# Feed-forward 0: small quantisation rows in PSUM, x first in VectorE's turn, statistics and factors in pairs, bank 0 shared

## What is computed

```
_GRID = [0.0, 0.5, 1.0, 1.5, 2.0, 3.0, 4.0, 6.0]; _MID = [0.25, 0.75, 1.25, 1.75, 2.5, 3.5, 5.0]
def fp4_quant_dequant(x):                 # blocks of 16 along the last dimension
    scale = max(max(|xb|) / 6, 1e-12)
    return _GRID[searchsorted(_MID, |xb / scale|)] * sign(xb) * scale
def fp4_linear(x, w): return quant(x) @ quant(w).T
gate, y = fp4_linear(x, w_gate), fp4_linear(x, w_up)      # 128 -> 352
out = fp4_linear(silu(gate) * y, w_down)                  # 352 -> 128
...
x = x + gelu(attention0(layernorm(x)));  x = x + ffn0(layernorm(x))
x = x + attention1(layernorm(x));        x = x + ffn1(layernorm(x))
```

## Time and profile before

| | us |
|---|---|
| median of 3 runs (1053.13 to 1054.89) | 1053.9 |
| the profiled execution | 1056.3 |
| its span | 1054.6 |
| PE busy in the span | 904.9 (86%) |
| DVE busy | 779.8 (74%) |
| ACT busy | 527.1 (50%) |
| POOL busy | 473.3 (45%) |

### The profile page before, as it was taken

How to read it: one execution, slowest core, us unless ns; L and a number is a source line. 1 busy time by engine, 2 the same in 40 slices (tenths; PEclk the granted TensorE clock), 3 DMA queues, 4 the chain that set the end, 5 groups by cost and what they waited for, 6 DMA issues and landing times. The chain is left out here.

```text
span 1054.6 us, 18304 instructions
## 1 busy us (share of the span) xinstructions
PE 904.9 (86%) x6457; PEld 588.5 (56%) x6457; DVE 779.8 (74%) x1505; ACT 527.1 (50%) x782; POOL 473.3 (45%) x643
## 2 busy tenths in 40 slices
PE   4799999995577667648999999988879999999997
PEld 3666777664455544524444444444356677667765
DVE  6788888875778888568878888888676666566742
ACT  3577777795234334444777767765732231323221
POOL 4122222225455556642655664545435433444344
PEclk9999999998688998776999999999999999999999
DMA  9100000000000000364444443410000000000000
GB/s 292 32 11 11 10 10 10 10 1 4 1 1 11 0 1 11 83 138 106 104 103 94 105 103 82 106 46 3 13 11 1 21 21 20 0 20 20 10 10 10
DMA packets 35639, 43.34 MB, mean 41 GB/s; under 512 B 4826, under 2 KB 27770, under 8 KB 35570
## 3 DMA queue, kind: packets, MB, share of 16 engines
q1 hardware_dynamic: 35569, 42.43, 16.5%
HBM read 21.21 MB, written 15.07 MB: 34 GB/s over the span
## 5 line engine op out<-in xcount | busy, mean ns | idle before, releaser
L1589 ACT ACTIVATE PT<-PS 128x1024 f32<-128x1024 f32 x160 | 162.8, 1022 | 68.3 <-PE PS L1373 68.1
L1643 POOL TENSOR_SCALAR_AFFINE_SELECT PT<-PT 128x256 f32<-128x256 f32 (+1 forms) x224 | 97.1, 449 | 133.1 <-ACT PT L1589 131.6
L2044 POOL TENSOR_TENSOR PRE_sb<-PRE_sb,VA 128x512 f32<-128x512 f32 x64 | 82.3, 1287 | 140.3 <-DVE PRE_sb L2110 140.2
L2007 ACT ACTIVATE sg_d<-PS 128x512 f32<-128x512 f32 x64 | 38.2, 597 | 176.7 <-PE PS L1111 176.7
L369 ACT ACTIVATE E<-PS,m 128x512 f32<-128x512 f32 x128 | 86.7, 684 | 40.9 <-PE PS L291 32.0
L2110 DVE TENSOR_TENSOR PRE_sb<-sg_d,PS 128x512 f32<-128x512 f32 x64 | 43.3, 686 | 79.1 <-ACT sg_d L2007 77.8
L1680 DVE TENSOR_REDUCE negm<-PS 128x2 f32<-128x1024 f32 x64 | 78.0, 1224 | 23.4 <-PE PS L1362 21.8
L496 DVE TENSOR_SCALAR E<-E 128x512 f32<-128x512 f32 x128 | 70.3, 549 | 33.6 <-ACT E L369 29.5
L1358 PE MATMUL PS<-kS,qS 48*128 48x384 bf16 (+3 forms) x512 | 75.0, 316 | 22.7 <-DVE negm L1680 8.5
L1388 PE MATMUL PS<-PT,VA 128*32 128x512 f32 (+3 forms) x1024 | 90.9, 452 | 1.4 <-POOL PT L1643 1.4
L406 POOL TENSOR_SCALAR Qs<-Qs 128x1024 f32<-128x1024 f32 x32 | 35.4, 1108 | 113.5 <-ACT Qs L357 113.5
(11 more groups left out here) (297 smaller groups left out, 2318.4 us busy)
## 6 DMA issues: line engine op xcount, KB each, us to landing
qk_rows<-parts SPq DMA_DIRECT2D x32, 192.0 KB, 2.8
qS<-qk_rows SPq DMA_DIRECT2D x32, 192.0 KB, 4.3
kS<-qk_rows SPq DMA_DIRECT2D x32, 192.0 KB, 4.6
xs_sb<-XN_sb SPq DMA_DIRECT2D x23, 256.0 KB, 2.3
qk_rows<-parts SPq DMA_DIRECT2D x32, 128.0 KB, 2.8
X_sb<-in_x_dram SPq DMA_DIRECT2D x8, 256.0 KB, 6.7
qk_rows<-parts SPq DMA_DIRECT2D x32, 64.0 KB, 2.4
out_dram<-X_sb SPq DMA_DIRECT2D x8, 256.0 KB, 2.3
```

The costliest lines, as they stand in the source:

```text
L1589: nc.scalar.activation(PT[:, quad % 2, u, :], PS[:, b:b + 2, :].rearrange("p b n -> p (b n)"), ACT.Exp).then_inc(exp_ready, 1)
L1643: nc.gpsimd.affine_select(out=v, in_=v, pattern=[[0, 4 if u == 4 else 2], [1, P]], compare_op=ALU.is_ge, fill=0.0, base=0, channel_multipl ...
L2044: nc.gpsimd.tensor_tensor(acts[:, s, f, :], acts[:, s, f, :], W[:, slot, s, :], ALU.mult).then_inc(weighted, 1)
```

## The change

- `am` and `inv` of each quantisation, for x and both hidden halves, lie in PSUM bank 1. The scale row `sc` stays in SBUF.
- The down products go to bank 0, half a bank each, and are kept by half (`keep_out(i, half)`). The bank is now used in turn by the attention sum, the transposed x, the two down halves and, in the last turns, the projections.
- VectorE's turn is `make_h(i, 0)`, `quantise_x(i + 1)`, `quantise_h(i, 0)`, `make_h(i, 1)`, `stats_x(i + 2)`, `stats_out(i - 1)`, `aggregate`, `quantise_h(i, 1)`. The eight `bn_aggr` of the two statistics stand together behind one wait.
- GpSimd rescales x in one piece ahead of `rescale_h(i, 0)`, and makes both factors with one chain of four instructions on 8 columns.
- TensorE's and ScalarE's orders are written anew, with `sum_att(i + 3)` a block earlier and functions of their own for the last two turns.

```diff
-    def __init__(self, sb, name, n):
+    def __init__(self, sb, name, n, small=None):
         self.y, self.pw, self.mg = (sb(name + m, [P, n]) for m in ("_y", "_pw", "_mg"))
-        self.am, self.sc, self.inv = (sb(name + m, [P, n // QB]) for m in ("_am", "_sc", "_inv"))
+        self.sc = sb(name + "_sc", [P, n // QB])
+        self.am, self.inv = small or (sb(name + m, [P, n // QB]) for m in ("_am", "_inv"))
...
+        nx, nh = NT * D // QB, 2 * I0 // QB
+
+        q_x = Scratch(sb, "qx", NT * D, [PS[:, 1, k * nx:(k + 1) * nx] for k in range(2)])
+        q_h = [Scratch(sb, "qh%d" % half, 2 * I0, [PS[:, 1, 2 * nx + (2 * half + k) * nh:2 * nx + (2 * half + k + 1) * nh] for k in range(2)])
+               for half in range(2)]
+        shift, vare = sb("shift", [P, 2, NT]), sb("vare_b", [P, 2, NT])
...
-                    pe.wait_ge(xqT_ready, i * 2 - 2)
+                    pe.wait_ge(xqT_ready, i - 1)
...
-            def turn_xq(i, part):
+            def turn_xq(i):
+                pe.wait_ge(xq_ready, i + 1)
+                if i < 2:
                     pe.wait_ge(att_kept, i + 2)
-                for t in (2 * part, 2 * part + 1):
+                else:
+                    pe.wait_ge(out_kept, i * 2 - 2)
+                for t in range(NT):
                     ins = nc.tensor.transpose(PS[:, 0, t * P:(t + 1) * P], xq[:, t, :], ident[:])
                 ins.then_inc(xq_turned, 1)
...
             def down(i, half):
-
-                pe.wait_ge(att_kept, i + 1)
-                if half == 0 and i > 0:
-                    pe.wait_ge(out_kept, i)
                 for t in (2 * half, 2 * half + 1):
-                    nc.tensor.matmul(PS[:, 1, t * P:(t + 1) * P], ident[:], X[:, i * NT + t, :], start=True, stop=False)
+                    nc.tensor.matmul(PS[:, 0, t * P:(t + 1) * P], ident[:], X[:, i * NT + t, :], start=True, stop=False)
                     if t % 2 == 0:
                         pe.wait_ge(hqT_ready, (i * 2 + half) * 2 + 2)
                     for r, (k0, kn) in enumerate(KT0):
-                        ins = nc.tensor.matmul(PS[:, 1, t * P:(t + 1) * P], hqT[0:kn, t % 2, r, :], g.wdT[0:kn, r, :], start=False, stop=(r == 2))
+                        ins = nc.tensor.matmul(PS[:, 0, t * P:(t + 1) * P], hqT[0:kn, t % 2, r, :], g.wdT[0:kn, r, :], start=False, stop=(r == 2))
                 ins.then_inc(down_ready, 1)
 
             def turn(i):
                 gate_up(i, 1)
...
                 if i > 0:
                     turn_h(i - 1, 1)
...
+                    pe.wait_ge(out_kept, i * 2 - 1)
                     down(i - 1, 1)
...
+                turn_xq(i + 1)
+                if i + 3 <= LAST:
+                    sum_att(i + 3)
+                gate_up(i + 1, 0)
                 turn_h(i, 0)
+                if i + 3 <= LAST:
+                    pe.wait_ge(att_kept, i + 4)
+                else:
+                    pe.wait_ge(xqT_ready, i + 2)
                 down(i, 0)
...
+            def turn_before_last(i):
+                gate_up(i, 1)
+                turn_h(i - 1, 1)
+                pe.wait_ge(out_kept, i * 2 - 1)
+                down(i - 1, 1)
+                turn_xq(i + 1)
+                pe.wait_ge(xqT_ready, NB)
+                pr.turn_x(pe, 0)
+                gate_up(i + 1, 0)
+                pr.project(pe, 0, 0, g.wq1, pr.q_ready)
+                turn_h(i, 0)
+                pe.wait_ge(pr.qf_ready, 1)
+                down(i, 0)
+
+            def last_turn(i):
+                gate_up(i, 1)
+                pe.wait_ge(out_kept, i * 2 - 1)
+                pr.project(pe, 0, 0, g.wk1, pr.k_ready)
+                turn_h(i - 1, 1)
+                pe.wait_ge(pr.kf_ready, 1)
+                down(i - 1, 1)
+                pe.wait_ge(out_kept, i * 2)
+                pr.turn_x(pe, 1)
+                turn_h(i, 0)
+                pr.project(pe, 1, 1, g.wq1, pr.q_ready)
+                pe.wait_ge(pr.qf_ready, 2)
+                down(i, 0)
+                pe.wait_ge(out_kept, i * 2 + 1)
+                pr.project(pe, 1, 1, g.wk1, pr.k_ready)
+                turn_h(i, 1)
+                pe.wait_ge(pr.kf_ready, 2)
+                down(i, 1)
...
             sum_att(0)
             sum_att(1)
             pe.wait_ge(w_kept, 4)
-            turn_xq(0, 0)
+            turn_xq(0)
             gate_up(0, 0)
-            turn_xq(0, 1)
-            for i in range(NB):
+            sum_att(2)
+            for i in range(LAST - 1):
                 turn(i)
+            turn_before_last(LAST - 1)
+            last_turn(LAST)
...
+            def keep_out(i, half):
+                own = X[:, i * NT + 2 * half:i * NT + 2 * half + 2, :].rearrange("p a d -> p (a d)")
+                act.wait_ge(down_ready, i * 2 + half + 1)
+                nc.scalar.activation(own, PS[:, 0, 2 * half * P:2 * (half + 1) * P], ACT.Copy).then_inc(out_kept, 1)
+
+            def keep_xq(i):
+                act.wait_ge(xq_turned, i + 1)
+
+                if i > 0:
+                    act.wait_ge(up_ready, i * 2)
+                nc.scalar.activation(xqT[:, :], PS[:, 0, :], ACT.Copy).then_inc(xqT_ready, 1)
...
             def turn(i):
                 silu(i, 1)
...
                 if i > 0:
                     keep_h(i - 1, 1)
+                    keep_out(i - 1, 1)
+                keep_xq(i + 1)
+                if i + 3 <= LAST:
+                    keep_att(i + 3)
+                silu(i + 1, 0)
+                keep_h(i, 0)
                 if i + 2 <= LAST:
...
+                    norm_x(i + 2)
+                keep_out(i, 0)
                 if i > 0:
                     norm_out(i - 1)
...
+            def factor(event, done, k0, k1):
+
+                ch = Steps(pool, g.pool_steps_b, event, 3)
+                both = [P, k1 - k0, NT]
+
+                wait_apart(pool, g.turns_g, g.factor_ready, NB + done - (k1 - k0))
+                wait_apart(pool, g.turns_g, g.stats_ready, NB + done)
+                ch.link(nc.gpsimd.tensor_scalar(vare[:, k0:k1, :], g.mv[:, k0:k1, :, 1], EPS_LN, 1.0, ALU.add, ALU.mult))
+                ch.link(nc.gpsimd.tensor_tensor(g.factor[:, k0:k1, :], vare[:, k0:k1, :], g.mhalf[:].unsqueeze(1).broadcast_to(both), ALU.pow))
+                ch.step(nc.gpsimd.tensor_tensor(shift[:, k0:k1, :], g.mv[:, k0:k1, :, 0], g.factor[:, k0:k1, :], ALU.mult))
...
             def rescale_x(i):
                 pool.wait_ge(x_rounded, i + 1)
...
+                ch = Steps(pool, tail_steps, i, 1)
+                rescale(nc.gpsimd, ch, xq[:, :, :].rearrange("p t (b k) -> p (t b) k", k=QB), q_x).then_inc(xq_ready, 1)
+                ch.end()
...
             for i in range(LAST):
+                rescale_x(i + 1)
                 rescale_h(i, 0)
-                rescale_x(i + 1)
-                if i > 0:
-                    factor(i * 2 + 1, 1)
-                if i + 2 <= LAST:
-                    factor(i * 2 + 2, 0)
+                if i == 0:
+                    factor(2, 3, 0, 1)
+                elif i + 2 <= LAST:
+                    factor(i + 2, i * 2 + 3, 0, 2)
+                else:
+                    factor(NB, 2 * NB - 2, 1, 2)
                 rescale_h(i, 1)
...
+            def aggregate(k0, k1):
+                norm.wait()
+                for k in range(k0, k1):
+                    for t in range(NT):
+                        norm.step(nc.vector.bn_aggr(g.mv[:, k, t, :], g.st[:, k, t, :]))
+                norm.wait()
+                dve.sem_inc(g.stats_ready, k1 - k0)
...
             for i in range(NB):
                 make_h(i, 0)
+                if i < LAST:
+                    quantise_x(i + 1)
                 quantise_h(i, 0)
                 make_h(i, 1)
+                if i + 2 <= LAST:
+                    stats_x(i + 2)
                 if i > 0:
                     stats_out(i - 1)
-                if i < LAST:
-                    quantise_x(i + 1)
-                if i + 2 <= LAST:
-                    stats_x(i + 2)
+                aggregate(0 if i + 2 <= LAST else 1, 2 if i > 0 else 1)
                 quantise_h(i, 1)
             stats_out(LAST)
+            aggregate(1, 2)
```

More of the change, by code:

```diff
@@ L172 @@
 QSTEPS = 6
-XQ_STEPS = 2 * NT + QSTEPS
 def attention0(nc, g, w):
@@ L721, in gate_up @@
             def gate_up(i, half):
-                pe.wait_ge(xqT_ready, i * 2 + half + 1)
+                pe.wait_ge(xqT_ready, i + 1)
                 if i > 0 or half > 0:
@@ L879, in turn, with turn_before_last @@
                     norm_out(i - 1)
-                if i + 2 <= LAST:
[L881 to L890, removed]
+            def turn_before_last(i):
+                silu(i, 1)
+                keep_h(i - 1, 1)
+                keep_out(i - 1, 1)
+                keep_xq(i + 1)
+                pr.keep_x(act, 0, 0)
+                silu(i + 1, 0)
+                pr.keep(act, 0, 0, pr.q_ready, pr.qf_ready)
+                pr.first_part(act, 0, 0, pr.qf_ready)
+                keep_h(i, 0)
+                keep_out(i, 0)
```

(38 more changed lines are left out.)

102 lines of the change are left out of this document (19 added, 83 removed).

## The result

The changed kernel takes 1028.8 us (1027.37 to 1031.25, 4 runs) against 1053.95 (1053.13 to 1054.89, 4 runs) before, timed on the same chip: ratio 0.9764 [0.9741, 0.9786]. The forecast was 1033.4, with a range of 1027 to 1042.

A forecast was written before the change was run, and what follows sets the result against it. VectorE, waiting on other engines and GpSimd's port holds, bounds feed-forward 0. Start and turn 1 +0.8, turns 2 to 5 −17.6, turn 6 −2.5, turn 7 −1.2 give −20.5 us: median 1053.9 becomes 1033.4, range 1027 to 1042.

The forecast's parts named there:

- (a): VectorE's wait before the output's statistics, for the output ScalarE keeps: 1.57 us a turn, to be gone.
- (b): VectorE's wait before the next product, for the up projection: 1.41 us a turn, to be gone.
- (c): Scale row and scaled product of the first hidden quantisation, held by GpSimd's rescales: 0.79 and 0.78 us lost, to be gone.
- (d): A further 0.3 us lost on VectorE, since the median scale row is 0.48; to be gone.
- one on the mask: VectorE's exponent mask of x (L160), held while GpSimd still rescales the previous hidden half: 0.35 us lost.
- The turn: VectorE's pieces in turns 2 to 5 sum to 17.1 us, plus the 0.35 hold; VectorE sets the turn at 17.4.
- Ends: Prologue and turns 0 and 1 together +0.8 us, turn 6 −2.5, turn 7 with the tail −1.2.
- Spares: Room before VectorE waits: x normalisation 1.3 us (0.6 with the dear power), up projection 3.8, TensorE's round 1.2.
- Dips kept: Rival: TensorE's clock stays at 0.87, its round is 18.6 us, five turns take 1.2 more each: 1039.4 us; chance 0.17.
- Touching PSUM costs: Rival: writing small rows to PSUM costs VectorE 0.9 us a turn in six or seven turns: 1039 us; chance 0.12.
- Holds moved to L160 to L162 in full: Rival: port waits move to VectorE's rounding side, 1.9 us a turn in place of 0.35: 1041 us; chance 0.12.
- The chain through bank 0 with a falling clock: Rival: bank 0's five users chain TensorE's round, 21.9 us at clock 0.74, 24.9 at 0.65: 1070 us; chance 0.05.

The follow-up runs named there:

- the sum in half: Changed kernel with the attention sum's products of two of the four tiles issued twice for blocks 3 to 7: 1033.6 us, ratio 0.9813.
- the doubled sum: Changed kernel with all eight products of the attention sum issued twice for blocks 3 to 7: 1031.6 us, ratio 0.9788.
- the run with the sum on GpSimd: Changed kernel with the rounding sum of x made by GpSimd in place of VectorE: 1033.2 us, ratio 0.9801.
- the kernel with x behind the half: Changed kernel with x quantised after the second product and rescaled after the first hidden half: 1061.1 us, ratio 1.0067.
- the statistics first: Changed kernel with the statistics of x directly behind VectorE's first product, ahead of the x quantisation, for i > 0: 1039.1 us, ratio 0.9846.

## Why the prediction was right, and where its terms were off

**The mechanism held.** VectorE sets the turn, the waits (a) and (b) of the earlier trace rows are gone, and the holds (c) and (d) of the earlier trace rows are gone but for one on the mask, predicted at 0.35 and measured at 0.31. VectorE works in 64.52 of the 68.06 us and waits in none of turns 2 to 5 for TensorE or ScalarE; the sum in half shows the other side, 0.9 us more on TensorE that leave the turn at 17.00.

**The turn, 17.4 forecast, 17.02 measured.** By the timeline above, the two products take 0.79 and 0.80 up to the next start (I had 0.92 each), the joint statistics 360.40 − 357.86 = 2.54 (2.74), x 3.90 with its hold (3.58 + 0.35), each hidden half 4.49 (4.47). Together 17.01. The terms that I mis-sized are the products (0.25 in the two: the next instruction starts before they end) and the joint statistics (0.20). Over four turns the error is 1.5 us.

**Ends.** Turn 1: I had 20.4, it took 18.30; the wait for the normalised x was 1.5 us and not 3. Turn 6: 16.91 against 16.3, since VectorE waited there once more for x, 1.15, behind the slow gate and up of turn 5. Turn 1's first product stands at 295.55, where I had 295.6, but that is luck. Attention 0, the same code in both kernels, ended 0.95 later in this execution (its last copy on VectorE starts at 250.72, before at 249.77). Without this, start and turn 0 added nothing, where I had 1.0. Turn 7 with the tail: −3.7 in place of −1.2, with 2.5 the largest error of the sum. TensorE's clock was 0.54 in 15 us of that tail before (433 to 448), and is 1.00 now in the stretch that holds the same products (400 to 422). What that is worth can be read between the last hidden transposes and the statistics of the last output. The work is the same; the first two lines are of before:

```profile
441.51 1.54 PE L739 MATMUL PS<-ident_sb,hh 128*128 128x128 f32 x6 [1.98 <-POOL hh L169]
...
448.03 0.87 DVE L104 BATCH_NORM_STATS2 st_sb<-X_sb 128x6 f32<-128x128 f32 x4 [10.28 <-ACT X_sb L815]
```

```profile
417.92 0.87 PE L744 MATMUL PS<-ident_sb,hh 128*128 128x128 f32 x6 [1.29 <-POOL hh L170]
...
422.02 0.87 DVE L1025 BATCH_NORM_STATS2 st_sb<-X_sb 128x6 f32<-128x128 f32 x4 [7.88 <-ACT X_sb L834]
```

It took 6.52 us and takes 4.10, so 2.4 of the 3.7 are the clock; from the start of turn 7 to those transposes it is 20.28 and 19.10, the 1.2 of the forecast. The forecast had no term for the clock here. I did not try what keeps it up.

**The median, 4.6 us under the forecast.** The sum had −20.5 for the stage. Between the two profiled executions the stage gave 27.1, counted from the end of attention 0. Of the 6.6 in excess, start and turn 1 have 3.1, turns 2 to 5 1.5 and the tail 2.5; turn 6 takes 0.6 back. Outside the stage, attention 0 took 0.95 more and the later stages 2.9 less (598.20 to 595.27), in all 29.0. The code behind the stage is the same, and over all the runs of this study it takes 595.3 to 600.3 (597.5 in the repeat of the changed kernel), so those 2.9 are no effect of the change. The medians differ by only 25.15, since the profiled execution before was 2.4 over its median and that of the changed kernel 1.4 under.

**Spares.** The normalisation of x had 0.9, not 1.3, because the power takes 1.65 for 8 elements. The power was in its bounds (1.02 to 2.04), and the spare was the tightest of the three. TensorE's was 1.2 by the forecast and 1.4 by the doubled sum, and the up projection was never waited for in turns 1 to 7.

**The rivals.** *Dips kept:* refuted in turns 1 to 4 and 6 (1.00), but one is left in turn 5 (0.80), where the forecast's own sign of it, gate and up at 4 us or more, appears at 5.03. The layout of the forecast has the attention sum in every turn and no wait over 1.3 on TensorE; turn 5 has no sum and a wait of 1.95. It costs about a microsecond, in turn 6. *Touching PSUM costs:* refuted. Over turns 1 to 5 the groups of the changed kernel read

```profile
L156 DVE TENSOR_REDUCE PS<-hh 128x44 f32<-128x704 f32 x10 | 8.9, 891 | 1.1 <-POOL hh L170 1.1
L159 DVE SCALAR_TENSOR_TENSOR qh_y<-hh,PS 128x704 f32<-128x704 f32 x10 | 8.9, 886 | 0.3
...
L157 DVE TENSOR_SCALAR qh_sc<-PS 128x44 f32<-128x44 f32 x10 | 2.0, 204 | 0.3
```

against 886 before for the reduction with its result in SBUF, and 891 and 186 at the least for the other two: +5, −5 and +18 ns. The reciprocal, which writes to PSUM, takes 436 against 428. All together is under 0.1 us a turn. The Trainium skill, VectorE: DVE Perf Modes, section "The TRN2 errata", has 62 cycles more for a PSUM source; the trace does not agree. *Holds moved to L160 to L162 in full:* refuted, 0.31; the run with the sum on GpSimd shows one of 0.73 on the magic product once GpSimd's rescale ends later. *The chain through bank 0 with a falling clock:* not in this kernel, but the kernel with x behind the half has it: turns of 21.76 at a clock of 0.76, where the rival put 21.9 at 0.74. It needed the missed wait on `hh[0]` too, which the forecast had overlooked and which costs 0.36 once where x goes first. The order of x is thus what keeps the rival away.

## What to carry to other kernels

Where VectorE's operand and GpSimd's meet in SBUF, move the one small row that is the second input of the wide instruction; the row of a one-input instruction gained nothing alone here, since the hold moved on to the next one, and 0.3 a turn on top of the other. Before reordering, list for each wait its spare, with those on overwritten buffers: the smallest (0.9 us here, on the normalised x) decided turn 6 and two of the runs. In a run that splits a joint step, set the waits of its users anew as well, or the run prices the wait and not the step. Moving work from the busiest engine to its neighbour gave nothing here, as the neighbour's rescale then ended inside the busiest engine's magic product.

## What the runs showed of the hardware

- GpSimd's power (1.02 us for 4 elements a partition and 1.65 for 8; 2.02 in all five turns with the statistics first) doesn't hold VectorE's scale row or its product with two SBUF inputs (0.19 and 0.89 beside it, with both rows in SBUF), while its rescales do (0.69 becomes 1.55). The Trainium skill, SBUF — State Buffer, section "Who interferes with whom", makes of the shared port pair an exclusive lock; the rows of the rescales agree, those of the power don't.
- It works the other way too: GpSimd's own instructions of 0.20 us take 0.36 to 0.73 when VectorE's mask, magic product, rounding sum or two-input product is at work.
- A small row in PSUM costs VectorE between 5 ns less and 18 ns more than in SBUF: 891 against 886 where the reduction writes it, 436 against 428 where the reciprocal reads SBUF and writes it, 886 against 891 where the product reads it, 204 against 186 where the scale row does.
- TensorE ran gate and up in 2.60 or in 5.03 us behind a wait of 1.94 and of 1.95 us, with 1.00 and 0.80 as the clock of the turn.
